# An attention kernel: V of eight heads as seven half-size block products kept in DRAM, and attention with its output projection as a stage of its own

## What is computed

```python
x = einsum('bct,bcd->bdt', x, cond_w[cond])      # one 32x32 mix per sequence
q, k, v = x @ Wq + bq, x @ Wk + bk, x @ Wv + bv   # 512 -> 4096 = 32 heads x 128
q, k = rms_norm(q), rms_norm(k)                   # over all 4096, times gq, gk
attn = softmax(q k^T / sqrt(128)) per head and sequence (32x32 scores)
x2 = x_residual + (attn v) @ Wo + bo              # 4096 -> 512
y = (causal long convolution of x2 by an SSM kernel + x2 * D) * mask
out = x2 + y @ Wf + bf + two low-rank terms       # A and B mixed over 16 LoRAs by a gate
```

## Time and profile before

| | us |
|---|---|
| runs shown | 841.64, 842.85, 843.61 |
| median | 842.85 |
| the profiled execution, its own time | 843.94 |
| its span in the trace | 842.1 |
| PE busy in the span | 825.3 (98%) |
| DVE, ACT, POOL busy | 589.2, 344.1, 466.0 (70%, 41%, 55%) |

### The profile page before, as it was taken

The page is one execution under the profiler, slowest core; times in us unless marked ns, Lnnn a source line. Parts: engine busy times, 40 slices in busy tenths (PEclk is TensorE's granted clock), DMA queues, the critical chain, the costliest instruction groups (busy, mean ns, idle before and its releaser), DMA issues.

```text
span 842.1 us, 15470 instructions
## 1 busy us (share of the span) xinstructions
PE 825.3 (98%) x6185; PEld 674.6 (80%) x6185; DVE 589.2 (70%) x632; ACT 344.1 (41%) x407; POOL 466.0 (55%) x433
## 2 busy tenths in 40 slices
PE   8799999999999999999999999999999999999998
PEld 7588877877888888878888888888888888888566
DVE  5878999999888888888646556366674767553441
ACT  4445555455555555555314233341422414222520
POOL 5987995545333333110099992769999998000410
PEclk9999999999999999999999999999999999999999
DMA  6125111111111111120011111131511011447501
GB/s 182 51 64 167 50 50 50 50 49 51 50 50 50 50 50 50 50 91 11 1 50 51 51 51 29 38 82 50 101 50 51 1 51 53 153 147 237 126 26 75
DMA packets 77529, 56.54 MB, mean 67 GB/s; under 512 B 25548, under 2 KB 60716, under 8 KB 77372
## 3 DMA queue, kind: packets, MB, share of 16 engines
q1 hardware_dynamic: 76560, 55.73, 22.2%
q10 hardware_dynamic: 940, 0.41, 0.2%
HBM read 52.32 MB, written 3.82 MB: 67 GB/s over the span
## 4 chain that ended last, share of the span: by engine, by line
PE 90%; DVE 4%; POOL 2%; issue 2%; ACT 1%; DVEq 0%; POOLq 0%
PE psum L652 15%; PE psum L654 15%; PE psum L653 15%; PE psum L705 12%; PE psum L707 11%; PE psum L706 11%; PE psum L808 7%; PE psum L740 2%; DVE sumsq L1363 1%; PE psum L917 1%; DVE qk_sb L1344 1%; PE psum L661 0%; DVE qk_sb L1351 0%; PE psum L668 0%; PE psum L682 0%
## 5 line engine op out<-in xcount | busy, mean ns | idle before, releaser
L1496 DVE TENSOR_TENSOR acc<-psum,acc 128x512 f32<-128x512 f32 x64 | 44.2, 691 | 98.4 <-PE psum L654 98.4
L407 POOL TENSOR_TENSOR w_raw<-w_raw 128x256 f32<-128x256 f32 x32 | 39.4, 1231 | 128.8 <-DMA w_raw<-in_wk 128.3
L705 PE MATMUL psum<-t_hi,w_hi 128*128 128x512 f32 x256 | 104.8, 409 | 5.5 <-DVE qk_sb L1355 3.4
L707 PE MATMUL psum<-t_hi,w_lo 128*128 128x512 f32 x256 | 100.6, 393 | 0.0
L706 PE MATMUL psum<-t_lo,w_hi 128*128 128x512 f32 x256 | 100.6, 393 | 0.0
L652 PE MATMUL psum<-wv_hi,mix_hi 128*128 128x512 f32 x256 | 100.4, 392 | 0.1
L654 PE MATMUL psum<-wv_hi,mix_lo 128*128 128x512 f32 x256 | 99.7, 389 | 0.0
L653 PE MATMUL psum<-wv_lo,mix_hi 128*128 128x512 f32 x256 | 99.6, 389 | 0.0
L1102 ACT ACTIVATE sq<-qk_sb 128x1024 f32<-128x1024 f32 x31 | 32.9, 1063 | 146.7 <-issue 141.9
L653 PE MATMUL psum<-wo_lo,attn_hi 128*128 128x512 f32 x224 | 87.1, 389 | 0.0
L652 PE MATMUL psum<-wo_hi,attn_hi 128*128 128x512 f32 x224 | 87.1, 389 | 0.0
(11 more groups left out here) (255 smaller groups left out, 1842.5 us busy)
## 6 DMA issues: line engine op xcount, KB each, us to landing
w_raw<-in_wq SPq DMA_DIRECT2D x32, 256.0 KB, 2.9
w_raw<-in_wk SPq DMA_DIRECT2D x32, 256.0 KB, 3.2
wv_raw<-in_wv SPq DMA_DIRECT2D x8, 1024.0 KB, 5.5
toep<-kpad_dram SPq DMA_DIRECT2D x2, 4096.0 KB, 14.2
wo_raw<-in_wo SPq DMA_DIRECT2D x7, 1024.0 KB, 5.3
x_nat<-in_x SPq DMA_DIRECT2D x4, 512.0 KB, 5.6
acc<-in_x SPq DMA_DIRECT2D x1, 2048.0 KB, 11.1
out_dram<-o_stage SPq DMA_DIRECT2D x8, 256.0 KB, 2.0
```

Of the source, the lines that this page charges most:

```text
L705: mm(bank(n), wh, hi[:, c, tok], start=(i == 0), stop=False)
L707: last = mm(bank(n), wl, hi[:, c, tok], start=False, stop=(i == 1))
L1496: v.tensor_tensor(acc[:, g, :], bank(6 + g % 2), acc[:, g, :], ALU.add).then_inc(acc_ok, 1)
```

## The change

Three things change together.

1. **V.** The 32 heads are taken as four groups of eight (1024 columns of Wv). Each group is computed as seven block products of half the size in features, tokens and columns (k halves, 512 tokens, 512 columns): 7 x 24 matmuls of 128x512 for eight heads in place of 2 x 96. All four groups are made first, in one stage of 28 products. GpSimd makes four sums of 128x1024 per group (`value_sums`) between its blocks of angles; ACT and DVE split seven operands of 128x1024 per group through a ring of four; DVE puts the results together (`value_post`, 14 additions of 128x1024 from PSUM per group). V of three groups is written to a DRAM tile `v_scr` (SP) and read back later in units of 2 MB; the last stays.
2. **Attention and projection** follow as a stage of eight units: a unit is one group of eight heads and one half of the tokens. A unit is `attend` with 32 program matmuls, then 4 token groups of 24 projection matmuls. The four sums stay in PSUM over the unit, so DVE has 4 additions to `acc` per unit, 32 instead of 64 in all. Wo is loaded and split by halves. The softmax of unit n+2 and the transposes of n+1 run beside unit n.
3. **Order elsewhere.** `acc` is loaded after the V stage and the eight additions of `bo` follow there (they were in the Q/K stage). GpSimd's clearing of `p_blocks` comes after the last `value_sums`. The LoRA mixing starts after the SSM kernel's matmuls, which stand before unit 2; its loads too. In head 0 DVE does four `post` parts ahead of the second half of the weight split. Four of the eight transposes of `acc` stand ahead of the last projection groups. The tiles are laid out anew in SBUF.

The core of the diff:

```diff
@@ sync
-            sp.wait_ge(tlo_ok, 4)
-            sp.dma_start(acc[:], x_rows).then_inc(acc_in, 16)
...
+            for t in range(3):
+                sp.wait_ge(wvlo_ok, 7 * t + 4)
+                load_v(t + 1, R_K1)
...
+                sp.wait_ge(wvlo_ok, 7 * t + 7)
+                sp.wait_ge(vs_ok, 4 * t + 4)
+                load_v(t + 1, R_K2)
+                sp.wait_ge(vc12_ok, 2 * t + 2)
+                spill(t, V_Q2, vq2_out)
...
+            sp.wait_ge(vp_mm, 2 * 28)
+            sp.dma_start(acc[:], x_rows).then_inc(acc_in, 16)
...
+            load_unit(2)
+            next_weights(1)
+            sp.wait_ge(kern_mm, 1)
             for c in range(KC):
                 sp.dma_start(la_nat[quadrant(c)], lora_a[...]).then_inc(la_in, 16)
@@ gpsimd
-            for g in range(G):
-                gp.tensor_tensor(acc[:, g, :], acc[:, g, :], bo_rows[:], ALU.add).then_inc(acc_set, 1)
-                combine(11 + g, (g + 1) % 2, 32 * ((11 + g) // 2) + 32)
...
+            def value_sums(t):
+                q1, q2, k1, k2 = (flat2(wv_raw[:, n]) for n in range(4))
+                s2 = value_raw(2, t)
+                pool.wait_ge(wvlo_ok, 7 * t + 1)
+                pool.wait_ge(wv_in[R_K1], 16 * t + 16)
+                gp.tensor_tensor(q1, q1, k1, ALU.subtract).then_inc(vs_ok, 1)
+                pool.wait_ge(vs_ok, 4 * t + 1)
+                pool.wait_ge(wv_in[R_K2], 16 * t + 16)
+                gp.tensor_tensor(k1, k1, k2, ALU.add).then_inc(vs_ok, 1)
...
+                    pool.wait_ge(vp_mm, 2 * (7 * t - 1))
+                gp.tensor_tensor(s2, k2, q1, ALU.subtract).then_inc(vs_ok, 1)
+                pool.wait_ge(vs_ok, 4 * t + 3)
+                pool.wait_ge(wvlo_ok, 7 * t + 2)
+                gp.tensor_tensor(q2, q2, s2, ALU.subtract).then_inc(vs_ok, 1)
...
+            reduce_angles(0, 16)
+            value_sums(1)
+            reduce_angles(16, 32)
+            reduce_angles(32, 48)
+            value_sums(2)
+            reduce_angles(48, 64)
+            reduce_angles(64, 67)
...
+            value_sums(3)
+            pool.wait_ge(wvlo_ok, 28)
+            gp.memset(p_blocks[:], 0.0).then_inc(blocks_zero, 1)
+            for g in (4, 5, 6, 7, 0, 1, 2, 3):
+                gp.tensor_tensor(acc[:, g, :], acc[:, g, :], bo_rows, ALU.add).then_inc(acc_set, 1)
@@ tensor
+            def value(t):
+                for j in range(7):
+                    pe.wait_ge(wvlo_ok, 7 * t + j + 1)
+                    for pair in range(2):
...
+                        value_pair(t, j, pair)      # 2 groups x 2 chunks x 3 matmuls
+                    if j == 0 and t == 0:
+                        head_scores(HEADS - 1, 1)
+                        norm_sums()
...
+            for n in range(7):
+                if n == 2:
+                    pe.wait_ge(tab_ok, 1)
...
+                attend(n)
+                project_first(n)
+                for g in range(HG):
+                    project_second(n, g)
@@ vector
+            def split_value(jj):
+                t, j = jj // 7, jj % 7
+                dve.wait_ge(wvhi_ok, jj + 1)
+                if j == 2:
+                    dve.wait_ge(vs_ok, 4 * t + 4)
+                v.tensor_tensor(flat2(ring_lo[jj % 4][:]), value_raw(j, t), ..., ALU.subtract).then_inc(wvlo_ok, 1)
...
+            for part in ("u4", "c12", "c22", "u3"):
+                post(part, 0, 0)
             dve.wait_ge(whi_ok, 1)
             first_lo(3, 7, 1).then_inc(wlo_ok, 1)
-            for part in ("u4", "c12", "c22", "u3"):
-                post(part, 0, 0)
...
+            split_value(2)
+            norms()
+            split_value(3)
+            for i in range(1, 28):
+                t, j = i // 7, i % 7
+                if j == 0:
+                    split_value(i + 2)
+                if i + 3 < 28 and j != 6:
+                    split_value(i + 3)
+                if i == 1:
+                    inverse_norms()
+                if j > 0:
+                    for pair in range(2):
+                        value_post(t, j, pair)
+                if i == 3:
+                    soft_max(0)
+                if i == 5:
+                    soft_norm(0)
+                if i == 25:
+                    spread(0)
+            soft_max(1)
+            split_o(0, 0)
+            for n in range(8):
+                attn_out(n)
+                if n % 2 == 0:
+                    split_o(n // 2, 1)
+                if n == 0:
+                    soft_norm(1)
+                if n + 1 < 8:
+                    spread(n + 1)
+                if n + 2 < 8:
+                    soft_max(n + 2)
+                if n == 7:
+                    dve.wait_ge(lora, 2 * (2 * NLORA - 1))
...
+                accumulate(n, (0,))
+                if n + 2 < 8:
+                    soft_norm(n + 2)
+                accumulate(n, (1,))
+                if n % 2 == 1 and n < 7:
+                    split_o(n // 2 + 1, 0)
+                accumulate(n, (2, 3))
```

More of the change, by code:

```diff
@@ new lines, in spill, with load_o, load_unit @@
+            def spill(t, part, done, groups=slice(0, HG)):
+                sp.dma_start(v_scr[t, :, part, 512 * groups.start:512 * groups.stop],
+                             v_sb[:, part, groups, :].rearrange("p g n -> p (g n)")).then_inc(done, 16)
+            def load_o(m, part):
+                quad = 2 * GROUP_ORDER[m] + part
+                tile = (wo_raw_a, wo_raw_b)[part]
+                sp.dma_start(tile[:], wo_rows[:, quad * QUAD:quad * QUAD + QUAD, :]).then_inc(wo_in[part], 16)
+            def load_unit(n):
+                group, half = UNITS[n]
+                sp.wait_ge(pv_mm, OCT * n)
+                sp.dma_start(v_sb[:, 0:2].rearrange("p b g n -> p b (g n)"),
+                             v_scr[group, :, 2 * half:2 * half + 2]).then_inc(vu_in, 16)
@@ L867, in _ @@
-            pe.wait_ge(tab_ok, 1)
-            pe.wait_ge(v_ok, 5 * G)
-            for h in range(SEQ):
-                i, q = h // 4, h % 4
-                last = mm(bank(0)[32 * q:32 * q + CA, CL * i:CL * i + CL], u_tab[:, :, 8 * q + i], expo[:, 0:CL, 8 * q + i],
-                          start=True, stop=True, tile_position=(0, 32 * q))
-            last.then_inc(kern_mm, 1)
-            attend(4)
-            pe.wait_ge(kern_ok, 1)
-            pe.wait_ge(wvlo_ok, 6)
-            for g in range(G):
-                value_group(5, g)
@@ new lines, in _, with attend @@
+            for t in range(4):
+                value(t)
+            def attend(n):
+                pe.wait_ge(p_ok, n + 1)
+                if n == 0:
+                    pe.wait_ge(vc12_ok, 8)
+                    pe.wait_ge(vc22_ok, 8)
+                    pe.wait_ge(vu3_ok, 8)
+                elif n == 1:
+                    pe.wait_ge(vc11_ok, 8)
+                    pe.wait_ge(vc21_ok, 8)
+                else:
+                    pe.wait_ge(vu_in, 16 * (n - 1))
+                for u in range(OCT):
+                    part = (1 if u < QUAD else 0) + (2 if n == 0 else 0)
+                    cols = slice(HD * (u % QUAD), HD * (u % QUAD) + HD)
+                    if n == 0 and u == 2:
+                        pe.wait_ge(vc21_ok, 7)
+                    if not (n == 0 and u < 4):
+                        pe.wait_ge(alo_ok, OCT * n + (u - 3))
+                    if n == 2 and u == 2:
+                        pe.wait_ge(kern_ok, 1)
+                    for g in range(HG):
+                        last = mm(bank(PV_BANK[u % 4])[:, P * g:P * g + P], v_sb[:, part, g, cols], p_blocks[:, u, g, :],
+                                  start=True, stop=True)
+                    last.then_inc(pv_mm, 1)
@@ new lines, in exp_scores, with attn_out @@
+            def exp_scores(n):
+                act.wait_ge(soft, n * 6 + 3)
+                sc.activation(sm_s[:], sm_s[:], ACT.Exp).then_inc(e_ok, 1)
+            def attn_out(n):
+                at_hi = attn(n)[0]
+                for u in range(OCT):
+                    act.wait_ge(pv_mm, OCT * n + u + 1)
+                    h = OCT * UNITS[n][0] + u
+                    sc.activation(at_hi[:, u, :], bank(PV_BANK[u % 4]), ACT.Identity,
+                                  bias=params[:, PARAM["bv"], h:h + 1]).then_inc(ahi_ok, 1)
@@ new lines, in _, with attn_out, split_o @@
+            soft_max(1)
+            def attn_out(n):
+                at_hi, at_lo = attn(n)
+                for u in range(OCT):
+                    h = OCT * UNITS[n][0] + u
+                    dve.wait_ge(ahi_ok, OCT * n + u + 1)
+                    v.scalar_tensor_tensor(at_lo[:, u, :], bank(PV_BANK[u % 4]), params[:, PARAM["bv"], h:h + 1],
+                                           at_hi[:, u, :].bitcast(F32), ALU.add, ALU.subtract).then_inc(alo_ok, 1)
+            def split_o(m, part):
+                hi, lo, raw = ((wo_hi_a, wo_lo_a, wo_raw_a), (wo_hi_b, wo_lo_b, wo_raw_b))[part]
+                dve.wait_ge(wohi_ok, 2 * m + part + 1)
@@ L1498, in quad @@
```

(23 more changed lines are left out.)

664 lines of the change are left out of this document (371 added, 293 removed).

## The result

| | before | after |
|---|---|---|
| median of five runs each, us | 842.82 | 848.80 (847.58 to 851.01) |
| ratio, 95% interval | | 1.0079 [1.0058, 1.0100] |
| span of the profiled execution, us | 842.1 | 846.4 |
| last projection (start of DVE's last addition to `acc`) | 780.0 | 772.7 |
| from there to the end | 62.1 | 73.7 |

The changed kernel is slower by 0.8%, outside the 0.2% that a measurement can tell. The forecast was 838.0, faster by 0.6%: it missed by 10.8 us and had the wrong sign, though the time lies inside the wide range given.

The account below looks back on a forecast made before the run. PE, holding nine tenths of the span, was taken as the bound. Terms -21.8 - 4.7 + 9.6 + 2.0 + 6.9 + 0.5 + 2.5 = -5.0 us on the 842.1 span gave a median of 838.0, range 826.5 to 850.5.

Parts of the forecast that it names:

- LoRA and the end: Last stage: transposed LoRAs only 8.8 us before the projections end, so late Toeplitz tile and b_all; +2.5 us.
- The matmuls and the Q/K stage: 96 fewer V matmuls, -21.8 us; Q/K stage with earlier post and no bias additions, -4.7 us.
- The V stage: PE waits 9.6 us for POOL's value_sums(2) at the third group's third product, plus 2.0 for slow clock.
- The switch: From V stage to first attend: PE stops 5.5 us for attn_lo, with slow clock; +6.9 us (bounds 3 and 9).
- My own second rival: Same as "POOL is the bound, and slower": late mixing counts once for b_all and, from 9.5 us, for the convolution.
- POOL keeps up: Rival, V stage: value_sums(2) in time, shorter switch stop, no loss at the end; 826 us, chance 0.20.
- POOL is the bound, and slower: Rival: DVE's two-operand work holds POOL fully; V waits 5 to 7 us more, mixing 8 more; 851, chance 0.22.
- DVE paces the units: Rival, attention and projection: units take 30 to 30.5 us instead of 28.9 while POOL mixes; 844, chance 0.08.
- the way through DRAM: Rival, units: a 2 MB V load comes late behind the Toeplitz tile or LoRA loads; 844, chance 0.04.

Follow-up runs that it names:

- e_split_first: Changed kernel with head 0's weight split put back ahead of the four post parts; 852.03 us, ratio 1.0120 to the kernel before.
- b_turn_late: Kernel before, with DVE's two transposes of the mixed LoRAs moved behind the fifth addition of the last quad; 852.96 us, ratio 1.0150.
- e_softmax_late: Changed kernel with soft_max(1) moved behind attn_out(0) and the split of Wo's second half; 851.26 us, ratio 1.0134 to the kernel before.
- e_la_early: Changed kernel with la_nat loaded right after POOL's last read of the angles, so LoRA mixing starts sooner; 835.18 us, ratio 0.9922 to the kernel before.
- e_sums_early: Changed kernel with value_sums(2) and value_sums(3) each one block of angles earlier; 848.02 us, ratio 1.0080 to the kernel before.
- c_la_switch: Changed kernel with the early la_nat load, POOL's sums early and a new order of DVE at the switch; 829.53 us, ratio 0.9835 to the kernel before.
- e_norms_late: Changed kernel with DVE's inverse_norms() behind the sums of the first group's second and third products; 847.44 us, ratio 1.0072 to the kernel before.
- c_best: Changed kernel with early la_nat load, later inverse_norms(), earlier POOL sums and p_blocks clearing, new DVE order at the switch; 825.75 us, ratio 0.9792 to the kernel before.

## Why the prediction was wrong

The step that failed is the term "LoRA and the end", +2.5 forecast and +11.6 measured. On the span the miss is 9.3 us (846.4 against 837.1), and 9.1 of it is this term. The other 1.5 of the 10.8 lie between span and median: the median was 2.4 us above the span, where I had taken it 0.7 above, rounded up.

**The matmuls and the Q/K stage held.** The last `post` part that opens the V stage (`c12`) came at 357.06 in place of 362.96: 5.9 us against the 4.7 forecast, of which e_split_first gave back 2.9 in its trace, against 3.2.

**The V stage: the sum held, the mechanism did not.** The first `attend` started at 528.72 against 533.2 less 4.7 = 528.5. `value_sums(2)` ended at 461.2 against 464.5 less 4.7 = 459.8. But PE arrived at the product that needs it at 461.9, some 10 us later than the 456.3 less 4.7 forecast, and so stopped 1.17 us there in place of 9.6, with the clock at 1.00 behind. It had lost the time at the start, in stops of 2.39 and 4.87 and half clock behind both, for which I had charged 3.1 us and then let them "disappear" in the later wait. What I had not priced there was `value_sums(0)` running against DVE's last sums of squares and norms. That the end agrees to 0.2 us is luck. So in part is 459.8: the text puts DVE's extra two-operand work at 9 us, where its own rates (0.22 against 0.16 over 82 us) give 4.9, and with that the sums would have been due some 3 us earlier.

**The switch held.** A stop of 4.87 (forecast 5.5) in the place named, with half clock behind it (the terms of this step add up to 7.1, not 6.9); unit 2's first matmul at 593.5 against 598.7 less 4.7 = 594.0; units of 29.1 from there (179.3 less 1.1 and 3.4, by six) against 28.9; the last projection at 772.7 against 772.0.

**"LoRA and the end" failed: +2.5 forecast, +11.6 measured.** The mechanism was the one named, a late Toeplitz tile and a late `b_all`; the term was mis-sized in three places. (1) The mixing took 157.8 us, not 154.7, so that the transposes ended 7.3 us and not 8.8 before the projections, and the Toeplitz load took 14.3, not 12.8: the convolution started 3.8 us late, not 0.7. (2) `b_all` was to be 4.7 us late on the schedule before and was 9.4: the kernel before wanted it 18.2 us after its last projection, and here it came 27.6 after (800.3 less 772.7). The slack had shrunk by 1.5 us more, and the way from the transposes to `b_all` took 34.9 us in place of 31.8, 1.7 of it in the sixteen writes. ACT's wait of 4.04 is near the 4.7 forecast only because the convolution itself ran 5.4 us late by then (3.8 and 1.6). And I let 1.2 us of ACT's wait reach PE, where nearly all of it did: 3.7 us more of stop at `y_tok` (4.28 against 0.54), because DVE's `y_lo` and `b_lo` are queued ahead of `y_tok`. (3) I charged no half clock: the first 64 matmuls of the convolution cost 1.6 us more, the last transposes of `y_tok` 0.9, the low-rank ones 1.6 (5.31 against 3.72). b_turn_late shows this term by itself, 11.5 us of tail.

The two late loads lie one inside the other. `b_all` waits in SP's queue for the transposes and for writes, and for nothing of the convolution, so by these rows a tile in time would have made ACT's wait 9.4 us long and not the tail much shorter. No run has the one without the other. My own second rival had added them, each us once for `b_all` and once for the convolution, which gives 5.7 + 2.2 = 7.9 for an end 7.3 us ahead; that it comes nearer to 11.6 than the forecast does not confirm it.

Of the rivals: "POOL keeps up" is out by the 9.06 us that DVE waited for `value_sums(2)`; "POOL is the bound, and slower" gave about the right total (851) by luck, since the longer V stage that it wanted is not there and the mixing took 3.1 us more than forecast, not 8; "DVE paces the units" is out for units 2 to 7 by their 29.1, but DVE is what V and unit 0 follow; the way through DRAM was in time, for no stop of TensorE in the units ends with a load of V.

The Trainium skill's rule (SBUF — State Buffer, "SBUF: two separate sides"), which the prediction had weighed, is seen in full in the pair 3.98 beside 3.80.

## What to carry to other kernels

When a stage gets shorter, ask for each thing that runs beside it when it must be ready at the end, and follow the last transfer through its own queue to its landing. What is late there is late for everything that stands behind its consumer, on each engine in turn, and the half clock behind the stops comes on top (4.1 us here, beside 7.5 of later starts and stops). Two transfers in one queue need not add up: ask which of them the end still waits for. A serial background engine should start its long job at the first moment its memory is free: 19 us of start, no work saved, were worth 1.6%. And where one engine's list is full, look for another place in the list before or between the operations that are waited for; behind the consumer, as in e_softmax_late, the operation only moved the stop.

## What the runs showed of the hardware

A DMA issue is not always short for the queue that makes it. Four loads of `lb_nat` (256 KB each) held SP's queue for 11.24 us in the changed kernel, 7.51 in e_la_early, and sixteen writes of 32 KB held it 17.37 (15.70 in the kernel before), where a load of V of 2 MB takes 0.34:

```profile
571.85 0.34 SPq L364 DMA_DIRECT2D v_sb<-v_scr_dram  x1
...
594.67 2.22 SPq L415 DMA_DIRECT2D la_nat<-in_lora_a  x4
596.93 11.24 SPq L417 DMA_DIRECT2D lb_nat<-in_lora_b  x4
608.21 1.68 SPq L364 DMA_DIRECT2D v_sb<-v_scr_dram  x1
```

What a stop costs in clock is not fixed by its length. After the stops of 4.87 us at the third product (4.87 to 5.02 in five traces with the norms at their old place: the changed kernel, e_la_early, e_sums_early, e_softmax_late, c_la_switch) the clock fell each time: it was 0.85 to 0.90 from 366 to 400. But at one of the small stops, the same matmul group in two kernels with the same DVE order there, it fell in one trace and not in the other (e_norms_late's line is the one at 402.02 above, 1.00 from 400 to 440). c_best:

```profile
403.29 0.47 PE L768 MATMUL psum<-ring_hi,t_hi 128*128 128x512 f32 x1 [1.92 <-DVE v_sb L1625]
...
400.00:440.00 40.00, 38.08 (x162) 31.09 (x161) 33.99 (x29) 11.26 (x11) 33.80 (x18) 0.96 0.43 160
```

What sets the two apart stays open.
